# A fused Mamba and mixture-of-experts kernel: the router's product with the weights' eight columns standing

## What is computed

```python
scores = jax.nn.softmax(xf @ gate_w.T, axis=-1)        # gate_w: 8 x 256
_, idx = jax.lax.top_k(scores, TOP_K)                  # TOP_K = 2
weights = jnp.take_along_axis(scores, idx, axis=-1) * ROUTE_SCALE
...
routed = jnp.einsum('ned,ne->nd', y, cw)
shared = jax.nn.silu(xf @ sg.T) * (xf @ su.T) @ sd.T
```

## Time and profile before

| | |
|---|---|
| Median of three runs | 5189.01 us (5183.5 to 5210.02) |
| The profiled execution, its time | 5185.9 us |
| Its span on the core | 5184.2 us |
| Busy: DVE / PE / POOL / ACT | 84% / 82% / 69% / 68% |
| PE weight loads busy | 57% |
| Mean granted TensorE clock | 0.915 of full speed |

### The profile page before, as it was taken

One profiled execution on the slowest core, in us unless ns is written; L12 is line 12 of the kernel. 1 busy time (PEld: TensorE's weight loads), 2 busy tenths in 40 slices (PEclk: granted clock), 3 DMA queues, 4 the chain that ended last, 5 costly groups with the idle time before them and its releaser, 6 DMA issues. The chain is left out here.

```text
span 5184.2 us, 75345 instructions
## 1 busy us (share of the span) xinstructions
PE 4226.3 (82%) x20862; PEld 2939.7 (57%) x20862; DVE 4336.0 (84%) x6189; ACT 3531.4 (68%) x6409; POOL 3559.4 (69%) x2235
## 2 busy tenths in 40 slices
PE   4778788788888888888888888888888888888874
PEld 2455555565555556555565555565565666656652
DVE  4899998988888898888888888888898888888742
ACT  4666666676666667767677667677767777776742
POOL 4666666666666667766777767677777786687853
PEclk6889998999899999898899999899999999999998
DMA  2122322343333323332333333333334443555662
GB/s 93 60 69 88 109 86 82 109 128 120 103 123 112 123 68 113 99 102 82 103 88 90 109 102 91 94 100 87 100 111 126 128 126 104 140 147 146 171 170 60
DMA packets 348416, 551.94 MB, mean 106 GB/s; under 512 B 39377, under 2 KB 196178, under 8 KB 347874
## 3 DMA queue, kind: packets, MB, share of 16 engines
q1 hardware_dynamic: 279026, 448.92, 28.2%
q0 software_dynamic: 47616, 65.17, 6.3%
q10 hardware_dynamic: 21360, 33.03, 1.7%
HBM read 432.78 MB, written 181.33 MB: 118 GB/s over the span
## 5 line engine op out<-in xcount | busy, mean ns | idle before, releaser
L568 POOL TENSOR_TENSOR dBx<-dtx,Bbc 128x1024 f32<-128x1024 f32 x1024 | 2430.5, 2422 | 714.9 <-DVE hs L1180 699.6
L1180 DVE TENSOR_TENSOR_SCAN hs<-ps,dBx 128x512 f32<-128x512 f32 x2048 | 2400.8, 1207 | 221.9 <-ACT ps L722 107.0
L722 ACT ACTIVATE ps<-dt,A 128x512 f32<-128x512 f32 x2048 | 1392.5, 689 | 595.1 <-DVE hs L1180 567.2
L935 PE MATMUL ps<-ident,hs 128*128 128x128 f32 x8192 | 1341.5, 303 | 495.7 <-DVE acc L1196 388.2
L935 PEld LDWEIGHTS ps<-ident,hs 128*128 128x128 f32 x8192 | 1037.0, 154 | 970.6 <-DVE acc L1196 617.8
L1196 DVE SCALAR_TENSOR_TENSOR acc<-ps,C_tok,acc 128x512 f32<-128x512 f32 x1792 | 1276.4, 738 | 263.2 <-PE ps L935 244.4
L624 POOL DMA_INDIRECT fx<-Y_slots,slots x248 | 393.8, 1588 | 105.8 <-issue 54.9
L603 POOL DMA_INDIRECT X_slots<-xs,slots x248 | 246.7, 995 | 263.2 <-DVE slots L1318 198.4
L1093 PE MATMUL ps<-xsT,wx 128*128 128x128 f32 x2432 | 324.6, 286 | 26.6 <-ACT xsT L814 26.6
L1169 DVE SCALAR_TENSOR_TENSOR xc<-ps,conv_w,xc 128x511 f32<-128x511 f32 (+2 forms) x384 | 285.9, 745 | 56.0 <-ACT xc L686 44.9
L1093 PEld LDWEIGHTS ps<-xsT,wx 128*128 128x128 f32 x2432 | 305.7, 201 | 44.6 <-issue 43.0
(11 more groups left out here) (206 smaller groups left out, 5967.8 us busy)
## 6 DMA issues: line engine op xcount, KB each, us to landing
Bbc<-B_scratch SPq DMA_DIRECT2D x512, 256.0 KB, 3.5
wx<-in_experts SPq DMA_DIRECT2D x304, 384.0 KB, 3.8
Y_slots<-zeros SPq DMA_DIRECT2D x228, 256.0 KB, 4.4
xin<-X_slots SPq DMA_DIRECT2D x304, 128.5 KB
Y_slots<-xin SPq DMA_DIRECT2D x304, 128.0 KB, 1.7
xt<-in_x SPq DMA_DIRECT2D x32, 512.0 KB, 4.0
shared<-xt ACTq DMA_DIRECT2D x31, 512.0 KB, 2.6
fx<-shared SPq DMA_DIRECT2D x31, 512.0 KB, 3.6
```

Of the source, the lines that this page charges most:

```text
L568: pool.tensor_tensor(dBx[u % 3][:], dtx[b % 2][:, 2 * h:2 * h + 2, :], Bbc[g % NBB][:, n % CH:n % CH + 1, :].broadcast_to([P, 2, T]), ALU. ...
L722: act.activation(psA[s % 2][:], dt[b % 2][:, j, :], ACT.Exp, scale=A[:, j, n:n + 1]).then_inc(s_dA, 1)
L935: i = pe.transpose(psH[w % 2][:, j * P:(j + 1) * P], hs[(n * CT + j) % NHB][:, t * P:(t + 1) * P], ident[:])
L1180: dve.tensor_tensor_scan(hs[s % NHB][:], psA[s % 2][:], dBx[s // 2 % 3][:, s % 2, :], 0.0, ALU.mult, ALU.add).then_inc(s_scan, 1)
```

## The change

The standing operand and the streaming one change places. `w_gate` (128x8) stands and `mT` (128x512) streams, in two products (one for each channel half) that leave the logits as 8 partitions by 512 tokens in `psG[1][0:8]`. ACT copies these to SBUF (`logits`, a free corner of the tile `few`), and PE turns them back with four transposes of 8x128 into the same 4 x 8 columns as before. DVE's work does not change. Two semaphores are new: ACT's copy waits for the two products (`s_gate_raw`), and PE's transposes wait for the copy (`s_logits`).

```diff
+        logits = few[B2:B2 + NE, D:D + T]
...
+        s_gate_raw, s_logits = sem("gate_raw"), sem("logits")
...
                         act.activation(mT[:, k, :], psG[k][:], ACT.Copy).then_inc(s_x2T, 1)
                     yield b
+                    act.wait_ge(s_gate_raw, b + 1)
+                    act.activation(logits, psG[1][0:NE, :], ACT.Copy).then_inc(s_logits, 1)
+                    yield b
                     act.wait_ge(s_route, b * NROUTE + 2)
...
                     pe.wait_ge(s_x2T, (b + 1) * KD)
+                    for k in range(KD):
+                        i = pe.matmul(psG[1][0:NE, :], w_gate[:, k, :], mT[:, k, :], start=(k == 0), stop=(k == KD - 1))
+                    i.then_inc(s_gate_raw, 1)
+                    yield b
+                    pe.wait_ge(s_logits, b + 1)
                     for t in range(NTB):
-                        for k in range(KD):
-                            i = pe.matmul(psG[1][:, t * NE:(t + 1) * NE], mT[:, k, t * P:(t + 1) * P], w_gate[:, k, :],
-                                          start=(k == 0), stop=(k == KD - 1))
+                        i = pe.transpose(psG[1][:, t * NE:(t + 1) * NE], logits[:, t * P:(t + 1) * P],
+                                         ident[B2:B2 + NE, B2:B2 + NE])
                     i.then_inc(s_gate_mm, 1)
```

More of the change, by code:

```diff
@@ L29 @@
     "ACT_post": [55.78, 60.79, 64.51, 67.98, 68.64, 81.05, 82.05, 82.05, 82.21, 82.21, 82.48, 82.48, 82.48, 84.37,
-        84.57, 84.94, 84.94, 86.67, 86.67, 87.25, 88.74, 90.2, 90.2, 97.75, 98.48, 98.57, 98.57, 100.3, 101.25,
-        102.44, 103.32, 104.24, 105.4, 116.62],
+        84.57, 84.94, 84.94, 86.67, 86.67, 87.25, 88.74, 90.2, 90.2, 97.75, 98.48, 98.57, 98.57, 100.3, 100.75,
+        101.25, 102.44, 103.32, 104.24, 105.4, 116.62],
     "ACT_pre": [-64.43, -64.18, -63.74, -60.5, -51.11, -50, -50, -50, -47.99, -34.01, -33.23, -33.23, -32.05, -31.84,
@@ L63 @@
         78.25, 80.39, 80.87, 81.19, 82.18, 85.81, 85.81, 86.11, 86.33, 86.52, 86.6, 87.44, 87.94, 88.1, 88.19, 89.15,
-        89.51, 89.51, 92.3, 92.51, 97.91, 98.52, 99.16, 100.51, 100.86, 102.64, 103.7, 103.82, 105.46, 105.71, 106.08,
-        106.08, 109.46],
+        89.51, 89.51, 92.3, 92.51, 97.91, 98.52, 99.16, 100.51, 100.86, 102.64, 103.17, 103.7, 103.82, 105.46, 105.71,
+        106.08, 106.08, 109.46],
     "PE_pre": [-33.55, -32.2, -29.99, -29.08, -25.16, -24.89, -23.09, -22.89, -20.13, -19.22, -15.7, -15.7, -15.25,
```

## The result

The changed kernel takes 5241.89 us (median of four runs, 5233.41 to 5246.53) against 5186.42 us for the kernel before in the same comparison. The ratio is 1.0096, with an interval of 1.0068 to 1.0124: it is about 50 us slower (the two medians lie 55 us apart). The forecast was 5243 us, in a range of 5198 to 5285. The profiled execution took 5238.66 us, with a span of 5236.9 us and the same mean granted clock as before, 0.915.

A forecast was written before the change was run, and what follows sets the result against it. A ring of ACT's decay, DVE's scan, PE's turn and DVE's weighing sets the pace, DVE slowest. 22 x (1.6 + 0.55) = 47, 9 x 1.3 = 12, and 1 make 60 us; nine tenths, 54, give 5243 us, range 5198 to 5285.

The forecast's parts named there:

- the upper bound of 2.6: Router products: four new records at the rate of a later slow product, eight records in 5.19 us.
- scan A: DVE's scan at 1770.24 in period 10, just after the router product; forecast to start 2.35 us late behind ACT's copy.
- The 0.77 us given back: DVE's idle time ahead of the convolution step in period 10, forecast to fall away and offset part of the stall.
- The two shapes: 22 ordinary periods built like 10 and 5, and 9 with DVE further behind, like period 19.
- the second shape: The 9 periods like 19, with DVE further behind: 1.3 us lost in each.
- The moved copy of `mT`: ACT's earlier copy delays the opening and PE's turns: 0 to 1.2 us, about 0.55 on average over 22 periods.
- Nine tenths arrive: Of 60 us summed delay, nine tenths, 54 us, reach the kernel's end; bounds 0 and all.
- the first shape: The 22 periods built like 10 and 5: 1.6 + 0.55 us lost in each.
- PE's half microsecond: The edit adds 0.5 us a period on PE, 17 us in all, hidden by PE's waits for DVE.
- the swallowed delay: Rival: DVE's 244.4 us of waits for PE absorb the delay, leaving 10 to 25 us; 5205 us, chance 0.18.
- the two clock rivals: TensorE's clock rises, 5156 us, chance 0.07; or falls, adding 43 us, 5286 us, chance 0.08.

The follow-up runs named there:

- the waiting copy: Kernel before, old product kept, with mT's second copy moved and an unused 8 x 512 copy on ACT waiting for the product: 5229.85 us, ratio 1.0063.

## Why the prediction was right, and where it was not

**What bounds the kernel** was read rightly: DVE's work stayed, its idle time grew.

**The products** were put at 1.96 us and took 1.88 in 25 of the 31 ordinary periods. In the first six they took 3.1, which lies outside the upper bound of 2.6: that bound was half of a slow product of eight records, not all of which need have been slow. The term that was missing is 6 x 1.1 us. It comes with the wait just ahead of the products and goes with it, as the run with `mT`'s copy back shows.

**The copy** took 0.58 us (0.6), **the transposes** 0.41 (0.42), and DVE didn't wait for them except in the last sequence, where its wait grew by 2.7 us (7.5 for 4.79) and 1.1 was foretold. **The stall ahead of scan A** in period 10 was 2.25 us (2.35), in period 19 1.4 us (1.4), as this row of the changed kernel shows:

```profile
3195.93 1.23 DVE L1189 TENSOR_TENSOR_SCAN hs<-ps,dBx 128x512 f32<-128x512 f32 x1 [1.37 <-ACT ps L724]
```

**The 0.77 us given back** came as foretold (18.9 us over the kernel).

**The two shapes** were real, but I took them for DVE being further behind. They are the two levels of TensorE's clock: in all nine periods of the second shape, and in no other ordinary one, the four token transposes ahead of the product took 0.60 us, at 2.4 GHz; elsewhere 0.7 to 1.06 us, in part or wholly at 1.2 GHz. The split of 22 and 9 held by luck as much as by reason (23 and 8 in the changed kernel).

**The moved copy of `mT`** was put at 0.55 us a period in 22 periods and 0.7 in the others, 18 us in the sum. Alone it cost 19. But taking it out of the changed kernel saved 19 us in one series and some 36 in the other. The slow product is not the reason, since the old product suffered from it more (3.42 us for 1.85, where the new ones took 3.09 for 1.88), and the periods with slow products were not the ones that became shorter. Nor did it work as I wrote: alone, it made DVE wait mainly for the tap, and in the changed kernel, where scan A is late anyway, this wait is small (66.7 us alone, 26.0 in the changed kernel). The 11 us that I wrote for it in two expectations were less than the sum on record had.

**Nine tenths arrive** is a step that the runs don't bear out. The gross stall was 75.7 us, near the 76 that 22 x (2.35 + 0.55) + 9 x 1.3 makes before anything is given back; the text's "about 50 us more" for the scan's wait was the net figure put in the place of the gross one. From there the ledger of the changed kernel reads: less 18.9 at the tap is 57, and 46 us of idle time were left at the end, eight tenths. But the doubled products arrived with 62 us for 45 us of longer waits, more than all, and the waiting copy on top of the moved `mT` with 14 us for 60. So 0.9 is no constant of this kernel.

**That the forecast lies 1 us off the median is luck.** By its own terms and nine tenths, four periods of the first shape and one of the second make 9 us for the first five periods, 18 and 8 of them make 44 us for the other 26, and 1 us is left for the end. The profiles show 20, 26 and 6 (two further profiles of the changed kernel give 20 for the first five periods and 30 and 34 for the others). The steps that were too small and the one that was too large cancelled.

**PE's half microsecond** was counted at nothing. The doubled transposes cost 16 and 21 us for 0.4 us a period, so the transposes of the change itself may well cost as much. So the 50 us can't all be the stall on ACT. Put one on the other, the runs give 19 us for the moved `mT`, 14 more with the waiting copy, and 17 more with the new products and their transposes. These steps go across two series, and each is uncertain by 10 us or more. That the last 17 us are PE's is argued, not shown.

**The rivals.** As wholes the swallowed delay and the two clock rivals are out: the kernel is 50 us slower, and the mean granted clock was 0.915 in both profiles. Yet the delay was swallowed in part, and the clock fell in part. Of the 60 us that the waiting copy added to the scan's wait, 51 were made up by shorter waits for the tap and for PE's turns. And the mean hides that the clock was lower in the first five periods (0.88 for 0.92), where the changed kernel lost 4.0 us a period, and a little higher in the others (0.94 for 0.93), where it lost 1.0.

The Trainium skill's rule on loads of weights ("TensorE: Matmul & The Clock Gate", LDWEIGHTS: time in proportion to the columns) is not borne out in the changed kernel either: a load of 8 columns shows 90 ns where 128 columns show 190, in the changed kernel's row (ns min/median/max):

```profile
L1033 PEld LDWEIGHTS ps<-mT,w_gate x128: 85/90/138, 290.4 to 5109.6; 128*8 128x8 f32 x128
```

**What stays open.** The copy's wait, the transposes and the moved `mT` each cost something alone, and their costs don't add up: with both moves on ACT undone the kernel was no faster than with both, with `mT`'s alone undone it was 19 and some 36 us faster, and with the copy of the logits alone late it was 42 us over before, against 50. Differences of 20 us between orders of the same work are not accounted for by the waits near the product. One candidate was not tested by itself: where in the period TensorE's clock changes its level. The 33 runs of the kernel before in the three series reach from 5166.51 us at a mean granted clock of 0.921 to 5203.65 us at 0.909, on the whole with shorter times at higher clocks. The kernel with both moves undone ran at 0.908 to 0.910 in all its runs, and that with `mT`'s copy back at 0.919 to 0.923. Whether the clock makes these differences or follows from them is not shown.

## What to carry to other kernels

A round trip that is put between a product and its reader (copy out, turn back) costs by the latency that the tightest engine sees, and not only by the work: here products of the same length (1.88 us for 1.85) came with a copy and a turn on top, and the copy held up an unrelated chain that stood behind it on its engine. Before placing an instruction that must wait, look at what is queued behind it and at when that was made before; if moving it only moves the idle time to the next reader, the trip itself is too long. Don't count added work on a full engine as free because that engine idles elsewhere: measure it by doubling it. And when an experiment carries two edits, run each of them alone too: here the copy alone seemed to cost 33 us, and 19 of them belonged to the edit that came with it.

## What the runs showed of the hardware

The old product of 8 streaming columns took 1.85 to 2.14 us before, and 3.42 us where the clock was at 1.2 GHz all through (the moved `mT` alone, period 3). The new one of 512 columns, with a quarter of the records, took 1.88 us at 2.4 GHz and 3.1 us where the clock was low for most of it. With one wait of 1.02 us of PE ahead of the product, in the six periods where it fell at the lower level, the granted clock was 0.59 of full speed during the products (period 5) instead of 0.90 without the wait. In period 27 of the changed kernel the same wait of 1.02 us began just after the clock had risen (0.50 until 4443.4 us, 1.00 from 4443.5), and the products took 1.88 us; a shorter wait of the same kind in a period where PE was at the higher level (0.57 us ahead of the products of period 19) left them at 1.88 us.
